# A split-precision attention product in a 16-block pipeline is rewritten as a full 32-bit one

## What is computed

```python
qp = (q @ Wq + bq).reshape(B, H, S, hd)       # 16 heads of 16, reshaped without a transpose
kp = k @ Wk + bk                              # one key and value head, 77 context rows
vp = v @ Wv + bv
att = jax.nn.softmax(jnp.einsum('bhsd,btd->bhst', qp, kp) * scale, axis=-1)
out = jnp.einsum('bhst,btd->bhsd', att, vp)
```

## Time and profile before

| | |
|---|---|
| median of 3 runs | 1291.59 us (1290.69 to 1292.88) |
| the profiled execution | 1290.6 us, its span 1288.8 us |
| busy: PE, weight loads, DVE, ACT, POOL | 1047.0 (81%), 905.3 (70%), 863.9 (67%), 591.6 (46%), 487.5 (38%) us |
| mean granted TensorE clock | 0.926 |
| the first stage | until about 420 us of the span |

### The profile page before, as it was taken

The page is one execution under the profiler, slowest core; times in us unless marked ns, Lnnn a source line. Parts: engine busy times, 40 slices in busy tenths (PEclk is TensorE's granted clock), DMA queues, the critical chain, the costliest instruction groups (busy, mean ns, idle before and its releaser), DMA issues. The chain is left out here.

```text
span 1288.8 us, 24770 instructions
## 1 busy us (share of the span) xinstructions
PE 1047.0 (81%) x7101; PEld 905.3 (70%) x7101; DVE 863.9 (67%) x2325; ACT 591.6 (46%) x1343; POOL 487.5 (38%) x695
## 2 busy tenths in 40 slices
PE   2798989898986958999999998377668888886665
PEld 1577877787865747999999997266557677765554
DVE  1588988888863536888888887556465555553454
ACT  0467777777773413434444442354324444443221
POOL 1445454545440013445445353277623333331000
PEclk9899999999997968999999999688879999998887
DMA  2866665757600411011011020134213222323332
GB/s 62 160 135 120 130 123 116 137 111 142 142 1 1 94 38 43 22 43 42 21 42 34 30 81 3 41 107 122 105 58 92 85 88 88 93 86 105 112 98 82
DMA packets 95477, 104.35 MB, mean 81 GB/s; under 512 B 18014, under 2 KB 87342, under 8 KB 95408
## 3 DMA queue, kind: packets, MB, share of 16 engines
q1 hardware_dynamic: 86144, 86.25, 27.8%
q0 software_dynamic: 6480, 16.85, 3.7%
q10 hardware_dynamic: 2784, 0.40, 0.2%
HBM read 38.38 MB, written 57.62 MB: 74 GB/s over the span
## 5 line engine op out<-in xcount | busy, mean ns | idle before, releaser
L430 POOL TENSOR_TENSOR prob_lo_hi<-prob,prob_lo_hi 128x616 f16<-128x616 f32 x64 | 95.8, 1496 | 129.3 <-ACT prob_lo_hi L506 129.2
L1643 POOL DMA_INDIRECT expert_out<-early_weights,aim x71 | 69.9, 985 | 153.4 <-DVE aim L1956 125.3
L735 PE MATMUL ps_scores<-kblock,qT 128*128 128x308 f32 x256 | 84.7, 456 | 11.1 <-ACT qT L490 5.8
L1185 ACT ACTIVATE f_hidden<-c_hidden,f_b 128x256 f32<-128x256 f32 x128 | 53.7, 471 | 68.2 <-PE c_hidden L1374 68.2
L1372 PE MATMUL c_mlp<-f_w_hi,f_hidden_hi 128*128 128x256 f32 x256 | 80.9, 316 | 3.9 <-DVE f_hidden_lo L1303 3.9
L2141 PE MATMUL m_gate<-x_weights_hi,m_zT_hi 128*128 x142 | 55.5, 391 | 33.5 <-DVE m_zT_lo L1961 32.8
L801 PE MATMUL ps_probT<-ident,prob_lo_hi 128*77 128x128 f32 x512 | 68.9, 279 | 15.4 <-DVE probT L380 12.8
L801 PEld LDWEIGHTS ps_probT<-ident,prob_lo_hi 128*77 128x77 f32 x512 | 59.2, 151 | 28.8 <-DVE probT L380 16.5
L1636 POOL DMA_INDIRECT sorted_rows<-m_z,slot_i x64 | 66.9, 1046 | 30.6 <-issue 19.9
L1372 PE MATMUL c_hidden<-y2T_hi,f_w_hi 128*128 128x256 f32 x256 | 77.1, 301 | 0.0
L643 DVE TENSOR_REDUCE mx<-ps_scores 128x8 f32<-128x616 f32 x64 | 50.7, 791 | 35.0 <-PE ps_scores L735 35.0
(11 more groups left out here) (331 smaller groups left out, 3503.7 us busy)
## 6 DMA issues: line engine op xcount, KB each, us to landing
sorted_rows<-no_row SPq DMA_DIRECT2D x15, 2322.0 KB, 13.9
m_z<-sorted_rows SPq DMA_DIRECT2D x71, 129.0 KB
early_weights<-expert_out SPq DMA_DIRECT2D x16, 512.0 KB, 5.7
early_weights<-expert_chunks SPq DMA_DIRECT2D x8, 640.0 KB, 6.9
x_all<-x SPq DMA_DIRECT2D x16, 256.0 KB, 13.1
combT<-combineT_all SPq DMA_DIRECT2D x16, 256.0 KB, 2.4
slT<-slots_all SPq DMA_DIRECT2D x16, 256.0 KB, 2.5
out<-x_all SPq DMA_DIRECT2D x8, 512.0 KB, 3.3
```

The source lines that it names most:

```text
L430: pool.tensor_tensor(prob2[:, u % 2, :, :, 0], prob[:, u % 2], prob2[:, u % 2, :, :, 1], ALU.subtract).then_inc(lo_done.sem, 1)
L735: return pe.matmul(out, lhsT, rhs, start=start, stop=stop)
L1185: last = act.activation(hf[:, q % 2, j, :], psH[:, q % 2, j, :], ACT.Relu, bias=fb1[:, c_:c_ + 1])
L1643: pool.indirect_dma_start(out=expert_out[:, :], in_=xo[:, i % 3, :], in_offset=None, out_offset=bass.IndirectOffsetOnAxis(ap=aim_i[:, i % ...
```

## The change

- `high_part` (ACT), `low_part` and `v_parts` (POOL) and `out_sum` (DVE) are gone, and with them the tiles `prob_lo_hi`, `vres`, `osum` and the signals between them.
- ACT writes V straight into `v1`, 32-bit, with one column of ones.
- `turn_p` transposes `prob` itself, and waits for `exps`. So `scores_out` of the next but one unit, which overwrites that half of `prob`, now waits for `turn_p`; before, it waited for `low_part`.
- `values` runs twice per block, each with 16 matmuls of 32 bits, with 17 columns each.
- `out_rec` and `out_scale` read PSUM, in two instructions each, and stand earlier in the list.

```diff
-                 (OUT, "values", 1), (MIX, "logitsT"), (OUT, "out_sum", 0), (OUT, "values", 2), (MID, "exps", 0),
-                 (MID, "scores_out", 1), (MID, "high_part", 0), (MIX, "neg_max"), (OUT, "out_sum", 1),
-                 (PRE, "ln1_apply"), (MIX, "neg_maxT"), (MID, "exps", 1), (OUT, "values", 3), (OUT, "out_sum", 2),
-                 (MIX, "combine"), (OUT, "out_sum", 3), (MID, "high_part", 1), (MIX, "turn_comb"), (MIX, "dispatch"),
-                 (MID, "scores", 2), (OUT, "out_rec"), (MIX, "normalise"), (MIX, "combineT_out"), (PRE, "kv"),
-                 (MID, "low_part", 0), (MIX, "disp_scale"), (MID, "turn_p", 0), (MID, "row_max", 2),
-                 (MIX, "turn_disp"), (OUT, "out_scale"), (MID, "low_part", 1), (MID, "scores_out", 2),
+                 (OUT, "values", 1), (MIX, "logitsT"), (MID, "exps", 0),
+                 (MID, "scores_out", 1), (MIX, "neg_max"), (OUT, "out_rec"), (OUT, "out_scale"),
+                 (PRE, "ln1_apply"), (MIX, "neg_maxT"), (MID, "exps", 1),
+                 (MIX, "combine"), (MIX, "turn_comb"), (MIX, "dispatch"),
+                 (MID, "scores", 2), (MIX, "normalise"), (MIX, "combineT_out"), (PRE, "kv"),
+                 (MIX, "disp_scale"), (MID, "turn_p", 0), (MID, "row_max", 2),
+                 (MIX, "turn_disp"), (MID, "scores_out", 2),
...
             def scores_out(b, u):
                 need(dve, mx_done, b, u + 1)
                 if u < 2:
-                    reuse(dve, lo_done, b, 3 + u)
+                    reuse(dve, pt_mm, b, 3 + u)
                 else:
-                    need(dve, lo_done, b, u - 1)
+                    need(dve, pt_mm, b, u - 1)
...
             def turn_p(b, u):
-                need(pe, lo_done, b, u + 1)
+                need(pe, exp_done, b, u + 1)
...
-                pairs = prob2[:, u % 2].rearrange("p g l two -> p g (l two)").bitcast(F32)
                 for g in range(UG):
-                    last = pe.transpose(psT[0:L, g, :], pairs[:, g, :], ident[:])
+                    last = pe.transpose(psT[0:L, g, :], prob[:, u % 2, g, :], ident[:])
...
             def values(b, w):
 
-                tile, half = w // 2, w % 2
-                bank = (psA, psB)[half]
+                bank = (psA, psB)[w]
                 if w == 0:
                     need(pe, pt_ev, b)
-                    need(pe, v_step, b)
-                if w >= 2:
-                    need(pe, osum_done, b, w - 1)
-                both = probT[:].rearrange("k h t g -> k h (t g)").bitcast(F16)\
-                               .rearrange("k h (q two) -> k h q two", two=2)
-                W = 3 * (HD + 1)
-                rhs = at(vpart, b).rearrange("k c d -> k (c d)")
-                for h in range(8):
-                    for part in (1, 0):
-                        last = mm(bank[:, h * W:(h + 1) * W], both[:, half * 8 + h, tile * P:(tile + 1) * P, part], rhs,
-                                  part == 1, part == 0)
+                    need(pe, v_out, b)
+                W = HD + 1
+                both = probT[:].rearrange("k h t g -> k h (t g)")
+                for h in range(G):
+                    last = mm(bank[:, h * W:(h + 1) * W], both[:, h, w * P:(w + 1) * P], at2(v1, b))
                 last.then_inc(pv_mm.sem, 1)
```

More of the change, by code:

```diff
@@ L233, in phase_a @@
         kblock = sb("kblock", [P, UG, L])
-        vpart = sb("vpart_all", [L, NB, 3, HD + 1], BF16)
-        vres = sb("vres", [L, 3, HD])
+        v1 = sb("v_and_one_all", [L, NB, HD + 1])
         z = sb("z", [P, TT, D])
@@ L282, in phase_a @@
         mu_diag_done, mu_bc_mm, mu_done = sig("mu_diag_done"), sig("mu_bc_mm"), sig("mu_done")
-        v_out, kv_mm, kb_done, v_step = sig("v_out"), sig("kv_mm"), sig("kb_done"), sig("v_step", 5)
+        v_out, kv_mm, kb_done = sig("v_out"), sig("kv_mm"), sig("kb_done")
         st1, mv1_done, rs1_step, z_done = sig("st1"), sig("mv1_done"), sig("rs1_step", 2), sig("z_done")
@@ L286, in phase_a @@
         sc_mm, mx_done, sub_done, exp_done = sig("sc_mm", 4), sig("mx_done", 4), sig("sub_done", 4), sig("exp_done", 4)
[L287 to L288 removed]
+        pt_mm, pt_ev, pv_mm = sig("pt_mm", 4), sig("pt_ev", 4), sig("pv_mm", 2)
         xb_done, o_step, x1_done = sig("xb_done"), sig("o_step", 2), sig("x1_done")
@@ L337, in phase_a @@
-                 (MID, "low_part", 2), (MID, "turn_p", 1), (MID, "row_max", 3), (OUT, "ln2_mean"),
+                 (PRE, "zT_out"), (OUT, "x1"), (MID, "scores", 3), (OUT, "ln2_stats"),
+                 (MID, "turn_p", 1), (MID, "row_max", 3), (OUT, "ln2_mean"),
                  (MIX, "slot_inputs"), (PRE, "queries"), (MID, "probT_act", 1), (MID, "scores_out", 3),
-                 (MID, "exps", 3), (OUT, "ln2_center"), (PRE, "kv_out"), (MID, "high_part", 3), (OUT, "rstd2"),
-                 (MID, "low_part", 3), (MID, "turn_p", 2), (PRE, "q_out"), (OUT, "ln2_scale"), (MIX, "comb_scale"),
+                 (MID, "exps", 3), (OUT, "ln2_center"), (PRE, "kv_out"), (OUT, "rstd2"),
@@ L341, in phase_a @@
+                 (MID, "turn_p", 2), (PRE, "q_out"), (OUT, "ln2_scale"), (MIX, "comb_scale"),
                  (OUT, "squares"), (OUT, "runit"), (PRE, "add_bv"), (MID, "probT_out", 2), (MIX, "slots_out"),
-                 (OUT, "unit"), (PRE, "v_parts")]
+                 (OUT, "unit")]
         @block.sync
@@ L392, in _ @@
             pool.memset(wv[:, :, HD:P], 0.0)
-            pool.memset(vpart[:, :, 0, HD:HD + 1], 1.0)
-            pool.memset(vpart[:, :, 1:3, HD:HD + 1], 0.0)
+            pool.memset(v1[:, :, HD:HD + 1], 1.0)
             pool.memset(no_row[:], 0.0)
@@ L426, in add_bv @@
                                    ALU.add).then_inc(xb_done.sem, 1)
[L428 to L449, removed]
             def rstd2(b):
@@ L468, in runit @@
                 pool.tensor_tensor(ru[:], ru[:], self.minus_half[:, 0:TT], ALU.pow).then_inc(ru_step.sem, 1)
-            run(pool, order, dict(rstd1=rstd1, add_bv=add_bv, low_part=low_part, v_parts=v_parts, rstd2=rstd2, runit=runit), NB)
+            run(pool, order, dict(rstd1=rstd1, add_bv=add_bv, rstd2=rstd2, runit=runit), NB)
         @block.scalar
@@ L494, in kv_move @@
                 need(act, kv_mm, b)
-                reuse(act, v_step, b)
                 reuse(act, kb_done, b)
                 act.copy(kT[:], psA[:, 0:L])
[L498 to L506, removed]
+                act.copy(at2(v1, b)[:, 0:HD], psA[0:L, P:P + HD]).then_inc(v_out.sem, 1)
             def probT_act(b, u):
@@ L577, in _ @@
             run(act, order, dict(kv_move=kv_move, zT_out=zT_out, q_out=q_out, exps=exps, probT_act=probT_act, unit=unit, disp_scale=disp_scale,
-                                 high_part=high_part, squares=squares,
+                                 squares=squares,
                                  xuT_out=xuT_out, combine=combine, dispatch=dispatch, combineT_out=combineT_out,
@@ L657, in probT_out @@
                 probT_part(dve, dve.tensor_copy, b, u)
[L659 to L664, removed]
             def out_rec(b):
-                need(dve, osum_done, b)
-                dve.reciprocal(orec[:], osum[:, :, :, HD]).then_inc(o_step.sem, 1)
+                need(dve, pv_mm, b)
+                for t, bank in enumerate((psA, psB)):
+                    last = dve.reciprocal(orec[:, t, :], bank[:, 0:G * (HD + 1)].rearrange("p (g d) -> p g d", g=G)[:, :, HD])
+                last.then_inc(o_step.sem, 1)
             def out_scale(b):
                 need(dve, o_step, b, 1)
[L672 to L675, removed]
+                for t, bank in enumerate((psA, psB)):
+                    last = dve.scalar_tensor_tensor(out=oprod[:, t], in0=bank[:, 0:G * (HD + 1)].rearrange("p (g d) -> p g d", g=G)[:, :, 0:HD],
+                                                    scalar=self.gates[:, 0:1], in1=spread(orec[:, t, :].rearrange("p (g a) -> p g a", a=1), 2, HD),
+                                                    op0=ALU.mult, op1=ALU.mult)
+                last.then_inc(o_step.sem, 1)
             def x1(b):
@@ L727, in _ @@
             run(dve, order, dict(kv_out=kv_out, ln1_stats=ln1_stats, ln1_apply=ln1_apply, row_max=row_max, scores_out=scores_out,
-                                 probT_out=probT_out, out_sum=out_sum, x1=x1, out_rec=out_rec, out_scale=out_scale, ln1_mean=ln1_mean, ln2_mean=ln2_mean,
+                                 probT_out=probT_out, x1=x1, out_rec=out_rec, out_scale=out_scale, ln1_mean=ln1_mean, ln2_mean=ln2_mean,
                                  neg_maxT=neg_maxT, comb_scale=comb_scale, ln2_stats=ln2_stats, ln2_center=ln2_center, ln2_scale=ln2_scale,
@@ L759, in kv @@
                 need(pe, ctx_in, b)
-                reuse2(pe, osum_done, b)
+                reuse2(pe, o_step, b)
                 for k in range(KD):
```

5 lines of the change are left out of this document (1 added, 4 removed).

## The result

The changed kernel takes 1428.7 us (median of four runs, 1421.0 to 1438.9), the kernel before 1292.2 us: 1.106 times as long, with a 95% interval of 1.099 to 1.114. The profiled execution took 1438.9 us, its span is 1437.2 us.

What follows compares the result with a forecast made beforehand. PE was taken to bound the first stage. Per turn +5.4 - 1.1 + 0.4 = +4.7 us, +75 over 16 turns, plus +80 for the clock, on 1290.6 gave 1446 us (1447 for the median); range 1351 to 1478.

Steps and rivals of the forecast that it cites:

- four bursts leave, two come, at 0.11 us per record: PE's `values` bursts: 1.6 us of 16-bit bursts leave, 64 records of 32 bits cost 7.0 us, net +5.4 per turn.
- the three waits: PE idle before the scores (0.22 us), the fourth transposes (0.88) and the turning of `xu` (0.87); together -1.1 per turn.
- the added wait: `scores_out` of the third unit waits for the first unit's transposes on PE instead of POOL: +0.4 us per turn.
- sum at an unchanged clock: First stage, clock level left aside: +4.7 us per turn, +75 us over the 16 turns with values.
- the clock: PE's clock falls in or behind the first burst; second burst and most logits run slower: +5 us per turn, +80 us.
- three rows: 16-bit against 32-bit load times (97, 190 ns) and the first logits record behind a `values` burst, placing a record near 0.11 us.
- The upper end: A short 32-bit record on PE with its 17 columns paid on top of the load: 0.125 us.
- the lower one: A record on PE with its load wholly hidden, as with 16-bit weights: 0.025 us.
- rival 2: The loads in PE's two bursts hide, 0.025 us per record, so the change is faster: 1280 us; chance 0.06.
- one comparison of two stretches: Clock fell to 1.2 GHz behind short `values` matmuls (59.60 to 63.00), but not behind less busy, long ones (854.90 to 858.30).
- rival 1: The clock holds at 2.4 GHz as PE runs without a break through the bursts: 1367 us, or 1383; chance 0.30.
- a choice between 1.8 and 8.8: Bounds of clock loss per turn: logits alone +1.8 us, both bursts and the logits +8.8; +5 was taken.

Runs made afterwards that it cites:

- the run with four parts: The changed kernel with 96 columns per product, with `prob` in four parts instead of two, so `scores_out` skips its block's transposes: 1.051 times the kernel before.

## Why the prediction was right

The sign, the place and the size came out: 1447 us were forecast and 1428.7 measured. For the profiled execution it was 1446 against 1438.9. By its terms, per turn:

| term | predicted | shown |
|---|---|---|
| four bursts leave, two come, at 0.11 us per record | +5.4 | +5.36 (2 x 3.49 - 1.62) |
| the three waits | -1.1 | -1.01 by idle time (0.22 + 0.74 in place of 1.97) |
| the added wait | +0.4 | +0.28 by the run with four parts |
| sum at an unchanged clock | +4.7 | +4.56 (26.25 - 21.69, with 96 columns) |
| the clock | +5 | +4.99 (31.24 - 26.25) |

The terms shown add up to 4.63, and 4.56 was measured. Two things that the prediction did not have nearly cancel in this. By the starts on PE, the way from the scores to the turning of `xu` is 143.24 - 140.31 = 2.93 us in place of 144.32 - 140.17 = 4.15, so the waits give back 1.22 and not 1.01. And the transposes of `dispT` and what follows them come about 0.17 us late, with 96 columns as well as in the run with four parts.

*What a record costs.* No row had a short 32-bit matmul, and the value was placed by three rows. The 0.08 us by which the first logits record was longer behind a 16-bit burst was the nearest of them: there the load had no long matmul before it. The distance came out at 0.112 us inside a burst. The upper end, with the columns on top of the load, fell with the run of 96 columns, and the lower one, the quick 16-bit passage (rival 2), with the change itself.

*The waits.* `ln2_scale` became short, and the 0.88 us vanished as worked out. That POOL's subtraction was the cause was only argued from an overlap in time; the wait put into the kernel before shows it.

*The clock.* That it would fall rested on one comparison of two stretches, and rival 1 was held at 0.30. The comparison could not carry more, since PE had also stood still ahead of two of the bursts there:

```profile
61.34 0.57 PE L735 MATMUL ps_small_a<-vpart_all,probT 77*128 77x51 bf16 x16 [0.58 <-DVE osum L662]
62.54 0.57 PE L735 MATMUL ps_probT<-vpart_all,probT 77*128 77x51 bf16 x16 [0.62 <-DVE osum L662]
```

So the few columns could not be told from the idle time by it. The runs with 96, 51 and 17 columns settle it. The size of 5 us was a choice between 1.8 and 8.8, and its picture does not hold. The prediction had the clock fall in or behind the first burst and stay down for the second burst and most of the logits. In six of the twelve turns (27.9 and 29.6 us) the first burst, the logits and nearly all of the second burst run at the full clock. The fall comes at the end of the second or just behind it, and costs 1.7 or 3.4 us over 26.25. In the other six the clock falls in or behind the first burst and stays down longer than the prediction had it, through the transposed logits and the turning of `comb` to the third scores. That costs 6.6 or 8.3 us (32.9 and 34.5). No turn loses the 5 us that were forecast for it. That the mean is 4.99 is luck, between two errors that cancel. By the windows the clock is 0.83 over the long steady stretch:

```profile
138.30:485.30 347.00, 335.58 (x1850) 291.31 (x1849) 186.16 (x387) 145.84 (x353) 44.09 (x78) 0.83 0.41 88
```

That is 0.34 of the time at the lower level, 0.34 x 31.24 = 10.6 us per turn, of which half, 5.3 us, is what the clock costs, in accord with the 4.99.

The profiled execution lies 7 us under its forecast. Of these, 2 us are the sum at an unchanged clock, which was 0.14 us too large in 16 turns. The rest, about 5 us, is not in the steady turns, so it lies in those at the ends, which were not worked out. The median lies lower still, because the four runs of the changed kernel differ by 18 us, and the profiled one is the slowest of them. Their granted clocks are 0.877 for the slowest and 0.893 for the fastest, so the clock's term is smaller in the others, by up to about 1 us per turn (18 us in 16 turns, an estimate).

## What to carry to other kernels

In the bursts here a 32-bit matmul with few moving columns costs what the load of its weights costs, and one of its records takes over four times as long as one with 16-bit weights (0.109 against 0.025 us). So splitting into 16-bit halves can pay even with twice the products and with work on three other engines. Count the load before the columns, and then look at the clock: a PE that is never idle can still drop to 1.2 GHz behind matmuls of few columns, and then the long ones around them pay too. Filling the columns under the load with a constant was worth 4.5% here, and interleaving short with long made it worse.

## What was not expected of the hardware

- More work made the kernel faster: 96 instead of 17 columns per product, 1360.9 us (1.056) against 1428.7 (1.106).
- Alternating eight short records with two long ones cost more than whole bursts did: turns of 33.3 us against 31.2, though at the full clock the alternation costs nothing (5.30 us either way). The clock came back at nearly the same place, but it never fell as late. Why was not tried.
- The same turn, with the same instructions, lost 1.7, 3.4, 6.6 or 8.3 us to the clock, depending on where in it the clock fell.
- One POOL subtraction beside it stretches a DVE instruction of 0.48 us to up to 1.74 us. A wait that keeps the two apart made the kernel before 1.1% faster.
